# Column numbers as FP32 in PSUM for the one-hots of builds and of late nodes

## The reference

```
norm_edge = dinv[src] * dinv[dst]            # dinv = deg ** -0.5
for W, b in ((W1, b1), (W2, b2), (W3, b3)):  # 256 -> 512 -> 512 -> 256
    h = h @ W
    msg = h[src] * norm_edge[:, None]
    h = relu(segment_sum(msg, dst) + b)
out = layernorm(x + h)
```

## Time and profile before

| | |
|---|---|
| time of a run, median of 3 | 2475.56 us (2475.43 to 2477.23) |
| the profiled execution's own time | 2475.53 us |
| its span, first to last instruction | 2473.7 us |
| busy time of PE | 2238.1 us (90%) |
| busy time of POOL | 1761.0 us (71%) |
| busy time of DVE | 847.8 us (34%) |
| busy time of ACT | 717.8 us (29%) |

### The profile page before, as it was taken

How to read it: one execution, slowest core, us unless ns; L and a number is a source line. 1 busy time by engine, 2 the same in 40 slices (tenths; PEclk the granted TensorE clock), 3 DMA queues, 4 the chain that set the end, 5 groups by cost and what they waited for, 6 DMA issues and landing times.

```text
span 2473.7 us, 33204 instructions
## 1 busy us (share of the span) xinstructions
PE 2238.1 (90%) x10765; PEld 1496.7 (61%) x10765; DVE 847.8 (34%) x1155; ACT 717.8 (29%) x1501; POOL 1761.0 (71%) x1768
## 2 busy tenths in 40 slices
PE   6977789999999998999998988898988799999998
PEld 6855577777777773444444444444444388888886
DVE  8887222222222212232333322322222224333333
ACT  6611222223232212222222222222221133333332
POOL 5177777777777767777777777777777766666663
PEclk9798899999999999999999999999999999999999
DMA  6436666666666667778777887777887665557773
GB/s 216 134 117 204 196 198 201 203 202 202 205 203 201 203 180 205 237 232 243 231 237 225 239 240 232 227 223 236 243 248 237 189 181 170 175 168 209 221 215 98
DMA packets 219959, 508.70 MB, mean 206 GB/s; under 512 B 38444, under 2 KB 106915, under 8 KB 219827
## 3 DMA queue, kind: packets, MB, share of 16 engines
q0 software_dynamic: 117216, 365.08, 51.3%
q1 hardware_dynamic: 83955, 109.08, 13.0%
q10 hardware_dynamic: 18656, 32.75, 4.4%
HBM read 433.60 MB, written 73.16 MB: 205 GB/s over the span
## 4 chain that ended last, share of the span: by engine, by line
PE 51%; POOL 19%; issue 15%; DMA 8%; POOLq 4%; DVE 2%; ACT 1%; ACTq 0%; DVEq 0%; SPq 0%
POOL rows L740 19%; PE ps_acc L1669 9%; PE ps_d L1669 7%; PE ps_h L1757 6%; DMA rows<-table,idx 6%; PE ps_T L1757 6%; PE ps_o L1718 6%; PE ps_acc L1665 5%; PE ps_d L1768 5%; POOLq L749 3%; PE ps_h L1709 3%; PE ps_d L1621 2%; DMA rows<-table_parts,idx 1%; PE ps_e L1739 1%; PE ps_l L1739 1%
## 5 line engine op out<-in xcount | busy, mean ns | idle before, releaser
L740 POOL DMA_INDIRECT rows<-table,idx x1249 | 1243.9, 996 | 461.6 <-issue 366.1
L1669 PE MATMUL ps_acc<-rows,sel 128*128 128x512 f32 (+2 forms) x1496 | 612.5, 526 | 91.1 <-DMA rows<-table,idx 72.5
L957 DVE SCALAR_TENSOR_TENSOR sel<-ps_e,firsts,dstT 128x1152 f32<-128x1152 f32 (+1 forms) x214 | 302.7, 1415 | 818.1 <-PE ps_acc L1669 309.6
L740 POOL DMA_INDIRECT rows<-table_parts,idx x483 | 475.7, 985 | 149.3 <-issue 139.8
L1669 PE MATMUL ps_d<-rows,sel 128*128 128x512 f32 (+2 forms) x1190 | 520.2, 549 | 56.2 <-DMA rows<-table,idx 56.2
L1669 PEld LDWEIGHTS ps_acc<-rows,sel 128*128 128x128 f32 x1496 | 279.9, 200 | 265.0 <-issue 138.0
L1669 PEld LDWEIGHTS ps_d<-rows,sel 128*128 128x128 f32 x1190 | 214.1, 193 | 213.0 <-issue 124.1
L1665 PE MATMUL ps_acc<-rows,sel 128*128 128x256 bf16 (+1 forms) x1533 | 246.0, 277 | 40.5 <-DMA rows<-table_parts,idx 25.6
L1718 PE MATMUL ps_o<-low,hT 128*128 128x512 f32 (+1 forms) x784 | 271.2, 489 | 0.9 <-ACT hT L1366 0.9
L1757 PE MATMUL ps_T<-pairs_r,rows_r 128*128 128x512 f32 x686 | 228.2, 449 | 9.6 <-ACT rows_r L1448 5.7
L1768 PE MATMUL ps_d<-big 128*128 128x256 bf16 x1470 | 227.0, 273 | 0.1
(11 more groups left out here) (192 smaller groups left out, 1660.8 us busy)
## 6 DMA issues: line engine op xcount, KB each, us to landing
rows<-table,idx POOLq DMA_INDIRECT x1249, 3.7
table<-made SPq DMA_DIRECT2D x49, 256.0 KB
acc<-table SPq DMA_DIRECT2D x49, 256.0 KB, 4.7
built<-big SPq DMA_DIRECT2D x30, 384.0 KB, 3.9
low<-built ACTq DMA_DIRECT2D x30, 384.0 KB, 3.8
built_bytes<-big SPq DMA_DIRECT2D x54, 192.0 KB, 5.1
low<-built_bytes ACTq DMA_DIRECT2D x54, 192.0 KB, 2.7
table_parts<-big SPq DMA_DIRECT2D x24, 384.0 KB
```

Of the source, the lines that this page charges most:

```text
L740: pool.indirect_dma_start(out=to, out_offset=None, in_=its[0:nodes, :], in_offset=bass.IndirectOffsetOnAxis(ap=idx[:, of, k:k + 1], axis=0 ...
L957: v.scalar_tensor_tensor(to[:, k:k + FRONT, :], numbers.unsqueeze(1).broadcast_to([P, FRONT, P]), firsts[:, bass.ds(t, 1)], dstT[:, bass.d ...
L1669: return mm(to[:, 0:w], sel[:, k, :], rows_of[phase][:, k, 0:w] if first is None else first, start=start, stop=stop)
```

## The change

The one-hots of the builds (`hot_j`, `hot_l`) and of the late nodes (`late_hot`, `first_hot`) are compared with column numbers that lie in PSUM as FP32. `numbers` serves three of them. `late_hot` takes `numbers` and adds the constant LATE in the same instruction, as a scalar_tensor_tensor. For `hot_j` a second set of 196 numbers, `j_numbers`, stands beside `numbers` in `ps_e[1]`. The bf16 tables `j_steps` and `p_steps` and the integers `late_ids` with their iota are gone. The digits `lo` and `hi`, the shapes, the outputs and the order of the work stay.

```diff
         few = sb("few", [P, P], I32)
-        late_ids = sb("late_ids", [P, P], I32)
...
-        away_flat = away[:, :, :, :].rearrange("p b c j -> p (b c j)")
-        j_steps = away_flat[:, 0:QUADS * PAIR].rearrange("p (j c) -> p j c", c=PAIR)
-        p_steps = away_flat[:, QUADS * PAIR:(QUADS + P) * PAIR].rearrange("p (j c) -> p j c", c=PAIR)
...
         numbers = ps_e[1][:, 0:P]
+        j_numbers = ps_e[1][:, P:P + QUADS]
...
-            nc.gpsimd.iota(late_ids[:, :], pattern=[[1, P]], base=LATE, channel_multiplier=0).then_inc(iota_done, 1)
...
-            v_.wait_ge(iota_done, 5)
+            v_.wait_ge(iota_done, 4)
...
             step(v.tensor_copy(numbers, few[:, :]))
-            v.tensor_copy(j_steps[:, :, :], j_ids[:, :].unsqueeze(2).broadcast_to([P, QUADS, PAIR]))
-            step(v.tensor_copy(p_steps[:, :, :], few[:, :].unsqueeze(2).broadcast_to([P, P, PAIR])))
+            step(v.tensor_copy(j_numbers, j_ids[:, :]))
...
-                v.tensor_tensor(late_hot, late_ids[:, :].unsqueeze(1).broadcast_to([P, SLOTS, P]),
-                                srcT[:, 0:SLOTS].unsqueeze(2).broadcast_to([P, SLOTS, P]), ALU.is_equal)
-                v.tensor_tensor(first_hot, few[:, :].unsqueeze(1).broadcast_to([P, SLOTS, P]),
+                v.scalar_tensor_tensor(late_hot, numbers.unsqueeze(1).broadcast_to([P, SLOTS, P]), float(LATE),
+                                       srcT[:, 0:SLOTS].unsqueeze(2).broadcast_to([P, SLOTS, P]), ALU.add, ALU.is_equal)
+                v.tensor_tensor(first_hot, numbers.unsqueeze(1).broadcast_to([P, SLOTS, P]),
...
-                v.tensor_tensor(hot_j, j_steps[:, :, :].unsqueeze(1).broadcast_to([P, PER_HALF // PAIR, QUADS, PAIR]),
+                v.tensor_tensor(hot_j, j_numbers.unsqueeze(1).unsqueeze(3).broadcast_to([P, PER_HALF // PAIR, QUADS, PAIR]),
                                 aside(lo, QUADS), ALU.is_equal)
-                v.tensor_tensor(hot_l, p_steps[:, :, :].unsqueeze(1).broadcast_to([P, PER_HALF // PAIR, P, PAIR]),
+                v.tensor_tensor(hot_l, numbers.unsqueeze(1).unsqueeze(3).broadcast_to([P, PER_HALF // PAIR, P, PAIR]),
                                 aside(hi, P), ALU.is_equal).then_inc(hots_ready, 1)
```

## The result

The changed kernel takes 2417.28 us (median of 4 runs, 2413.47 to 2421.05) against 2475.73 us of the kernel before (2475.43 to 2477.23): a ratio of 0.9764, 95% interval 0.9748 to 0.978. That is 58.4 us off, where 50.7 were predicted, and inside the predicted range. The profiled execution is the slowest of the four, 2421.05 us with a span of 2419.3, so the trace shows 54.4 us of the gain (2473.7 less 2419.3).

The account below looks back on a forecast made before the run. POOL's issue of gathers was taken to set the pace in phases 1 and 0, with PE close behind in phase 0. 34 + 17.5 + 0.2 - 1 = 50.7 us off 2475.5 gave 2425 us, between 2416 and 2447; overall range 2413 to 2455.

Parts of the forecast that it names:

- The stall and its cause: Gathers stall beside DVE compares with two SBUF inputs; PSUM numbers return 35.6 us to POOL in phase 1, 23.3 in phase 0.
- The rival that it has another cause: Gathers stay stalled because something other than their read is held off; only 0.2 us won, 2475 us; chance 0.03.
- the rival that the stall lasts as long as the new pair: POOL held until the end of 5.71 us, 2.71 us more for each of 56 pairs: 2620 us; chance 0.04.
- How much reaches the end: Of POOL's returned time, 34 us (26 to 36) shorten phase 1 and 17.5 us (9 to 23) phase 0.
- the first rival: Stalls go but the path doesn't follow: half of phase 1, a quarter of phase 0 gained, 2456 us; chance 0.10.
- The price of the slower compares: Each of 56 pairs 2.71 us longer on DVE, mostly hidden before take_sum; loss 1 us, between 0 and 7.
- One sign: If the forecast is right, PE's waits for rows in phase 1 fall from 80 to about 45 us.
- The sum: 34 and 17.5 us from stalls, 0.2 from one-time changes, less 1 for slower compares: 50.7 us off.

Follow-up runs that it names:

- FP32 in SBUF: Changed kernel with the builds' FP32 column numbers moved from PSUM to SBUF, same type, shapes and rate: 2613.03 us.
- the longer pair: Changed kernel with a reduction of 2156 columns from PSUM between hot_j and hot_l in every pair: 2416.59 us; with two such reductions, 2456.83 us.
- the late nodes' compares: Changed kernel with both compares of the builds back on bf16 numbers in SBUF, so only the late nodes' read PSUM: 2470.96 us.
- `hot_l` alone: Changed kernel with hot_j back on bf16 numbers in SBUF, while hot_l still reads PSUM: 2469.82 us.
- the second comparison: The changed kernel run again without an edit, beside the kernel before: 2415.82 us against 2472.2 us.
- `take_apart` through PSUM: Changed kernel with take_apart's rows copied to PSUM two tiles at a time, except the last three, and its two mid-phase-1 calls halved: 2404.17 us.

## Why the prediction was right, and where its sizes were off

**The stall and its cause** were right. The rival that it has another cause falls with FP32 in SBUF against FP32 in PSUM; the rival that the stall lasts as long as the new pair falls with the 0.95 us gathers of the profile after. Two details of my picture were wrong. A gather waits not until 0.31 us before the end of the pair but until the end of the one instruction that holds it, and takes some 0.82 us from there. With `hot_j` alone holding it, the two readings give the same end in the kernel before, so the sum of the stalls, 58.9 us, stood (56.0 in the 55 pairs I counted and 2.9 over the late compares; the trace has 58.0 in all 56, and 2.9). And the earlier trace rows don't speak for two SBUF inputs as the cause in all four gathers: two of them are held by the cast of line 1092, which has one SBUF input (last section). The gather beside line 957 in the earlier trace rows starts 0.61 us after it, not 0.7; nothing rests on that.

**How much reaches the end** was mis-sized in phase 1. I took 95% of 35.6 us, 34. Over the whole phase the stretch falls from 50.6 to 12.3 us, by 38.3 (my 870 us held 35 of its 36 pairs; the trace has 37.4 us of stretch over all 36, and `take_apart` stretches some 1 us less in this execution), and 37.2 and 38.4 us arrive in the two profiles. The reason given, that POOL has no idle time there and PE slack, was right: the length of phase 1 is 786 x 1.25 us plus the stretch in the kernel before (982.5 + 50.6), in the changed one (982.5 + 12.3, measured 996.1) and without any stretch (983.0). So the first rival, that the path doesn't follow, falls. In phase 0 I took 17.5 of 23.3 us; 15.7 and 20.3 arrive. There PE does become the bound in some windows, as predicted: in four of the seven places between 405 and 562 us where POOL waits, the profile names PE as what it waits for. Yet I had given PE too little slack, since I counted only its waits of the earlier trace rows. The same view has another row, for the first windows:

```profile
PE ps_acc L1669 <- DMA rows<-table,idx: 23.1, 13, 3.4
```

So PE waited 48.7 us for rows there and not 25.6, and its upper value is 804 - 48.7 = 755 us, not 778. Of PE's own waits the one for `take_sum` grows, from 14.5 us to 21.7 and 30.4 in the two profiles; but the execution with the larger one loses less of the gain, so it isn't what keeps the rest of the 23.3 us from arriving.

**The price of the slower compares** was right in itself and wrong in its effect: I took 1 us of loss, and the runs show none. I had looked for the cover in the wait before `take_sum` (2.94 us in the tightest window). That wait is used up in places, as the timeline after shows, and still nothing is lost, because behind it lies PE's wait for rows: a late one-hot takes its time from that, and the longer pair shows how far it goes.

**One sign was wrong in size.** I expected PE's waits for rows in phase 1 to fall from 80 to some 45 us; they fell to 60.5. Of the 37.2 us by which the whole phase is shorter, PE's waits for rows give 21.3 (from 103.2 to 81.9), and 16.0 come from PE's own busy time (929.51 to 913.46) for nearly the same number of matmuls (2836 and 2833). The granted clock of the stretch is 0.98 of full speed (2.4 GHz) and was 0.97; a rounded hundredth is some 9 us by my estimate (0.01 of 930 us). The kernels with the late nodes' compares and with `hot_l` alone, in which the pairs still hold the gathers, have PE busy for 921.8 and 919.9 us in that stretch, so about half of the 16.0 us comes and goes between executions. Whether the clock is all of the rest wasn't tried.

**The sum**: 34 + 17.5 + 0.2 - 1 = 50.7 us predicted; in the profiled executions some 37 to 38 and 16 to 20, 54.4 and 59.4 in all; 58.4 by the medians, and 56.4 in the second comparison (2472.2 less 2415.82). Phase 2 is unchanged within a microsecond or two: 501.2 us from the last `take_sum` of phase 1 to the end before, 502.4 after.

## What to carry to other kernels

A stall is priced by what it holds up, not by the engine that makes it. Here DVE does 150 us more work and the kernel is 58 us faster, since in each pair a compare with two SBUF inputs had held POOL, which sets the pace. The Trainium skill ("VectorE: DVE Perf Modes", section "Rules for kernel authors") advises bf16 from SBUF for the rate of a tensor_tensor. The rows agree on the rate (1784 ns against 3415), while the kernel goes the other way. Look in the trace for a group whose longest instruction is far above its median, and ask what runs beside the long ones.

To find how much slower an engine off the path may get, follow its lateness to the wait that PE has anyway, not only to the engine's own idle time; a dummy instruction of known length, in one or two runs, measures it.

## What the runs showed of the hardware

A gather that starts during a DVE compare with two SBUF inputs is held until that instruction ends, and ends 0.81 to 0.83 us after it; it is let through between two such compares that follow each other closely. That holds for `hot_j` at 3.42 us (FP32) as at 1.78 us (bf16), and for the late nodes' int32 compares of 2.55 us in other tensors. So in this kernel the slower form from SBUF is the worst of all: two held gathers for each pair instead of one, 2613 us. A DVE instruction of 3.42 us with one SBUF input and one from PSUM holds none: the longest gather over the 56 pairs of the changed kernel took 0.96 us. The compares hold a gather only at its start: each of the 56 gathers that `hot_j` held in the kernel before had started after it, 0.06 to 1.26 us into it, and of the 44 already running when a `hot_j` began it held none.

One SBUF input isn't always few enough. The cast of `take_apart` reads one SBUF tensor and writes another; in the kernel before, beside the gathers of the earlier trace rows:

```profile
1294.79 1.75 DVE L1092 CAST pairs_r<-big 128x3072 fp32r<-128x3072 f32 x1
...
1590.84 1.75 DVE L1092 CAST pairs_r<-big 128x3072 fp32r<-128x3072 f32 x1
```

The gather that starts in the first cast ends 0.81 us after it, like one beside a compare. The gather at 1590.34 had been running for 0.50 us when the second cast began; it takes 2.37 us and ends 0.12 us after the cast, so a cast can hold a running gather too. In the kernel with `take_apart` through PSUM, the copy into PSUM and the cast out of it stretched none of the 24 gathers that started in them.
